# An integer cross attention regrouped by tile of queries inside a twelve-stage decoder kernel

## What is computed

```python
q = (x @ Wq + bq).reshape(1, B * N, H, hd)
kv = (cond @ Wkv + bkv).reshape(1, -1, 2, H, hd)
k, v = (kv[:, :, 0], kv[:, :, 1])
q = jnp.transpose(q * scale, (0, 2, 1, 3))        # k and v likewise
q = _fq_sym(q, axis=-1)                           # x / s rounded, clipped to +-127, times s
k = _fq_sym(k, axis=-1)                           # s = max|x| / 127 over the 16 columns
v = _fq_sym(v, axis=2)                            # over all tokens, per column
attn = softmax(einsum('bhqd,bhkd->bhqk', q, k))
attn = _fq_unsigned(attn, axis=-1)                # in steps of 1/255 of the row's maximum
out = einsum('bhqk,bhkd->bhqd', attn, v)
return out @ Wp + bp
```

## Time and profile before

| | us |
|---|---|
| median of 3 runs | 2005.1 (2003.45 to 2008.04) |
| profiled execution | 2004.22 |
| its span | 2002.9 |
| mean granted TensorE clock | 0.823 of full |
| stage `l1_cross`, from the start of its norm to the start of the next stage's | 642.3 to 953.8 |

### The profile page before, as it was taken

The page is one execution under the profiler, slowest core; times in us unless marked ns, Lnnn a source line. Parts: engine busy times, 40 slices in busy tenths (PEclk is TensorE's granted clock), DMA queues, the critical chain, the costliest instruction groups (busy, mean ns, idle before and its releaser), DMA issues. The chain is left out here.

```text
span 2002.9 us, 26899 instructions
## 1 busy us (share of the span) xinstructions
PE 1505.2 (75%) x8561; PEld 1049.0 (52%) x8564; DVE 1264.7 (63%) x3283; ACT 813.5 (41%) x2155; POOL 707.0 (35%) x969
## 2 busy tenths in 40 slices
PE   4899954799997558886884793035678769948998
PEld 3566643688886312223553462012456559935665
DVE  3677775455555778985335426988688679962222
ACT  1244421243342268883225213311577558821111
POOL 1488830166553436663001002425455312200000
PEclk8899986899998755556886896558799979968999
DMA  5000002100000035662200002010000020000000
GB/s 195 22 7 7 1 12 89 41 7 6 1 1 1 0 64 106 106 107 42 90 1 0 0 1 87 0 37 23 31 1 1 17 111 2 2 1 1 1 0 21
DMA packets 98380, 62.20 MB, mean 31 GB/s; under 512 B 88896, under 2 KB 93376, under 8 KB 96448
## 3 DMA queue, kind: packets, MB, share of 16 engines
q1 hardware_dynamic: 98240, 60.48, 11.3%
HBM read 38.44 MB, written 1.05 MB: 20 GB/s over the span
## 5 line engine op out<-in xcount | busy, mean ns | idle before, releaser
L101 PE MATMUL banks<-arena_a,normed_t 128*128 128x512 f32 (+3 forms) x736 | 282.5, 534 | 11.7 <-PEq L2983 11.7
L421 POOL TENSOR_TENSOR lut_weights<-lut_weights,arena_b 128x536 f32<-128x536 f32 x128 | 179.1, 1399 | 193.0 <-DVE arena_b L411 183.1
L101 PEld LDWEIGHTS banks<-arena_a,normed_t 128*128 128x128 f32 x736 | 140.3, 211 | 123.8 <-issue 120.4
L580 POOL TENSOR_SCALAR work<-work,small 128x256 f32<-128x256 f32 (+1 forms) x384 | 178.8, 483 | 73.9 <-DVE small L572 73.9
L101 PE MATMUL banks<-arena_a 64*128 64x512 bf16 (+1 forms) x384 | 161.7, 540 | 17.6 <-ACT arena_a L1483 9.3
L1483 ACT ACTIVATE arena_a<-banks,work 128x1024 uint8<-128x1024 f32 x128 | 154.0, 1203 | 39.3 <-DVE work L1428 28.7
L1426 DVE TENSOR_REDUCE work<-banks 128x1 f32<-128x1024 f32 x128 | 155.5, 1215 | 19.9 <-PE banks L101 19.9
L1513 POOL TENSOR_SCALAR arena_a<-arena_a 128x1024 bf16<-128x1024 uint8 x128 | 133.0, 1045 | 84.8 <-DMA arena_a<-arena_a 83.3
L107 PE MATMUL banks<-identity,work 128*128 128x128 f32 x968 | 133.3, 279 | 16.8 <-DVE work L1086 11.2
L560 ACT ACTIVATE work<-banks,small 128x256 f32<-128x256 f32 (+1 forms) x258 | 115.2, 458 | 62.3 <-DVE small L547 58.2
L107 PEld LDWEIGHTS banks<-identity,work 128*128 128x128 f32 x968 | 112.9, 145 | 31.5 <-DVE work L1086 12.2
(11 more groups left out here) (398 smaller groups left out, 3414.0 us busy)
## 6 DMA issues: line engine op xcount, KB each, us to landing
arena_a<-in_L3f_wg SPq DMA_DIRECT2D x1, 4096.0 KB, 12.4
arena_b<-in_lut_idx SPq DMA_DIRECT2D x8, 268.0 KB, 2.8
arena_b<-in_L_wqn SPq DMA_DIRECT2D x1, 2048.0 KB, 12.4
arena_b<-in_L_wo SPq DMA_DIRECT2D x1, 2048.0 KB, 16.5
arena_a<-in_L_wq SPq DMA_DIRECT2D x1, 2048.0 KB, 7.6
arena_a<-in_L_wo SPq DMA_DIRECT2D x1, 2048.0 KB, 13.6
arena_a<-arena_a SPq DMA_TRANSPOSE x128, 2.5
arena_a<-in_L_wgu SPq DMA_DIRECT2D x1, 2048.0 KB, 8.9
```

The source lines that it names most:

```text
L101: ins = t.matmul(out, lhs_t, rhs, start=start and i == 0, stop=stop and i == n - 1)
L421: g.tensor_tensor(o, o, lut_t[j % 2], ALU.add).then_inc(*summed.up(c * LUT + j))
L580: ins = g.tensor_scalar(e[:, c], e[:, c], A.rl[n % 2][:, 2 * hh + i:2 * hh + i + 1], 0.0, ALU.mult, ALU.add)
```

## The change

Only the stage `l1_cross` changes.

- `at(n)` is now `n // H, n % H`: a unit is still one tile and one head, but all 16 heads of one tile come first, then the next tile. All eight pairs of keys (`kt`) stay in SBUF; the queries are turned by tile (`query_slots`, two buffers).
- The output of a tile is made inside the loop. Behind the tile's last unit e: DVE norms all 16 heads in one operation at its step e + 8, PE turns the tile at e + 10, ACT copies it at e + 10, PE projects it at e + 12, DVE adds it to the residual and takes its statistics at e + 13. `OutputOfAll` and two of the four barriers are removed. The value scales are put on the rows of the projection weight instead of on the output.
- Head: PE makes the keys first, then turns the normed residual (ACT alone copies it), then makes queries, then values; DVE, ACT and POOL take keys first too. POOL spreads the queries behind all of its key work. Quotients are written as int16 and so rounded by the conversion, in place of the two operations with the large number. POOL's spreading now also clips the queries.
- All eight transposes of keys and the first of queries are issued by SP in front of the barrier; inside the loop one transpose of queries is issued per tile.
- Biases of keys, queries and output are added by a product of one row of ones with the bias row, behind the products of the weights.

The core of the diff:

```diff
         def at(n):
-            return n // (2 * NT), n // 2 % NT, 2 * (n // (2 * NT)) + n % 2
+            return n // H, n % H
+        def ended_at(n):
+            return n // H if 0 <= n < N and n % H == H - 1 else None
+        def projected(bank, x_t, b, w_, bias):
+            for i in range(TB):
+                ins = products(t, bank[:, i * D:(i + 1) * D], [(lhs(x_t, b * TB + i, k), w_(k)) for k in range(KH)] + [(ones[0:1, :], bias[0:1, :])])
+            return ins
...
         def tensor():
+            for b in range(NB):
+                projected(banks[b].f, ctx_t, b, lambda k: W["wkv4"][:, k * 512:k * 512 + D], W["bk4"]).then_inc(*ts.up(s, "k", b))
+            for b in range(NB):
+                t.wait_ge(*(yield normed_v, s, b))
+                t.wait_ge(*(yield normed_a, s, b))
+                token_turns(banks[4 + b].f, nf[:, b * CB:(b + 1) * CB], id_f).then_inc(*turned.up(s, b))
+            for b in range(NB):
+                t.wait_ge(*(yield xt_a, s, b))
+                projected(banks[4 + b].f, xt, b, lambda k: W["wq4"][:, k * D:(k + 1) * D], W["bq4"]).then_inc(*ts.up(s, "q", b))
...
-            for n in range(N + 7):
+            for n in range(N + 14):
...
+                if (i := ended_at(n - 10)) is not None:
+                    t.wait_ge(*(yield normed_o, s, i))
+                    turns(t, id_f, [(out_bank(i)[:, D + j * P:D + (j + 1) * P], oc[i % 2][:, j * P:(j + 1) * P]) for j in range(KH)]).then_inc(*o_in_psum.up(s, i))
+                if (i := ended_at(n - 12)) is not None:
+                    t.wait_ge(*(yield o_t_a, s, i))
...
+                    products(t, out_bank(i)[:, 0:D], [(ot[i % 2][:, j * P:(j + 1) * P], wp[j]) for j in range(KH)] +
+                             [(ones[0:1, :], W["bp4"][0:1, :])]).then_inc(*out_made.up(s, i))
...
         def vector():
+                v.tensor_tensor(heads(ki[b % 2]), heads(banks[b].f), each(r1), ALU.mult).then_inc(*vs.up(s, "k", b))
+                if b >= 2:
+                    v.wait_ge(*(yield as_, s, "split", b - 2))
+                v.tensor_scalar(kv[b % 2], ki[b % 2], 127.0, -127.0, ALU.min, ALU.max).then_inc(*vs.up())
+                v.tensor_tensor(heads(kv[b % 2]), heads(kv[b % 2]), each(s1), ALU.mult).then_inc(*vs.up(s, "keys", b))
...
+                if (i := ended_at(n - 8)) is not None:
+                    v.wait_ge(*(yield exped, s, n - 8))
+                    v.reciprocal(rl[i % 2], ls[:, i * H:(i + 1) * H]).then_inc(*vs.up())
+                    v.wait_ge(*(yield mixed, s, n - 8))
+                    v.tensor_tensor(heads(oc[i % 2]), heads(out_bank(i)[:, 0:D]), each(rl[i % 2]), ALU.mult).then_inc(*normed_o.up(s, i))
+                if (i := ended_at(n - 13)) is not None:
+                    v.wait_ge(*(yield out_made, s, i))
+                    x_i = x[:, i * D:(i + 1) * D]
+                    v.tensor_tensor(x_i, out_bank(i)[:, 0:D], x_i, ALU.add).then_inc(*added.up(s, i))
+                    v.bn_stats(stat[:, 6 * i:6 * i + 6], x_i).then_inc(*vs.up())
+                    v.bn_aggr(mv[:, 2 * i:2 * i + 2], stat[:, 6 * i:6 * i + 6]).then_inc(*vs.up())
...
         def scalar():
+            for b in range(NB):
+                a.wait_ge(*(yield turned, s, b))
+                a.copy(*copied_t(b, banks[4 + b].f)).then_inc(*xt_a.up(s, b))
+            for b in range(NB + 1):
+                if b < NB:
+                    for n in range(3):
...
+                    as_.all(s, "split", b)
+                if b:
+                    z = b - 1
+                    a.wait_ge(*(yield ts, s, "v", z))
+                    a.activation(vtf[:, z * 512:(z + 1) * 512], banks[z].f, ACT.Identity, bias=W["bv4"][:, z // 2:z // 2 + 1]).then_inc(*as_.up(s, "v", z))
+            for k in range(KH):
+                a.activation(v16[k], vtf[:, k * 1024:(k + 1) * 1024], ACT.Identity, scale=rv[:, k:k + 1]).then_inc(*as_.up(s, "rounded", k))
...
+                if (i := ended_at(n - 10)) is not None:
+                    a.wait_ge(*(yield o_in_psum, s, i))
+                    a.copy(ot[i % 2], out_bank(i)[:, D:2 * D]).then_inc(*o_t_a.up(s, i))
...
         def sync():
-            yield MEET
-            turn_pair(0)
+            sp.wait_ge(*(yield as_, s, "split", NB - 1))
+            turn_keys(0)
+            sp.wait_ge(*(yield gs, s, "spread", 0))
+            turn_queries(0)
+            for pr in range(1, H // 2):
+                turn_keys(pr)
+            yield MEET
             for n in range(N):
-                if n % (2 * NT) == 4 and pr + 1 < H // 2:
...
-                    turn_pair(pr + 1)
+                if h == 4 and i + 1 < NT:
+                    if i:
+                        sp.wait_ge(*(yield scored, s, i * H - 1))
+                    turn_queries(i + 1)
```

More of the change, by code:

```diff
@@ L1369, in vector @@
[L1369 removed]
+            yield from norm_vector(s, nf)
             for b in range(NB):
[L1371 to L1399 removed]
@@ L1408, in vector @@
[L1408 to L1419 removed]
+                s1, r1 = sc[b][:, 0:32], sc[b][:, 32:64]
@@ new lines, in vector @@
+                v.wait_ge(*(yield ts, s, "k", b))
+                v.tensor_reduce(s1, heads(banks[b].f), AX.X, ALU.max, apply_absolute_value=True).then_inc(*vs.up())
+                v.wait_ge(*vs.now())
+                v.tensor_scalar(s1, s1, 1.0 / 127.0, 1e-8, ALU.mult, ALU.max).then_inc(*vs.up())
+                v.wait_ge(*vs.now())
+                v.reciprocal(r1, s1).then_inc(*vs.up())
+                v.wait_ge(*vs.now())
+                v.tensor_tensor(heads(ki[b % 2]), heads(banks[b].f), each(r1), ALU.mult).then_inc(*vs.up(s, "k", b))
@@ L1458, in scalar @@
-            for b in range(NB):
-                for n in range(3):
-                    if n == 0:
-                        a.wait_ge(*(yield vs, s, "keys", b))
-                    else:
-                        a.wait_ge(*(yield gs, s, "rest", b, n - 1))
-                    for i in range(TB):
-                        a.copy(slots4(kx, b * TB + i)[:, :, :, n, :], pairs(kt_[b % 2] if n else kv[b % 2], i)).then_inc(*as_.up())
-                    as_.all(s, "part", b, n)
-                as_.all(s, "split", b)
@@ new lines, in scalar @@
+            a.wait_ge(*(yield loaded[4], "all"))
+            for b in range(NB + 1):
+                if b < NB:
+                    for n in range(3):
+                        if n == 0:
+                            a.wait_ge(*(yield vs, s, "keys", b))
+                        else:
+                            a.wait_ge(*(yield gs, s, "rest", b, n - 1))
+                        for i in range(TB):
+                            a.copy(key_slots(b * TB + i)[:, :, :, n, :], pairs(kr[b % 2] if n else kv[b % 2], i)).then_inc(*as_.up())
+                        as_.all(s, "part", b, n)
+                    as_.all(s, "split", b)
[3 more added lines that the diff above has]
+                    a.activation(vtf[:, z * 512:(z + 1) * 512], banks[z].f, ACT.Identity, bias=W["bv4"][:, z // 2:z // 2 + 1]).then_inc(*as_.up(s, "v", z))
```

323 lines of the change are left out of this document (108 added, 215 removed).

## The result

The changed kernel takes **1985.8 us** (1985.2 to 1986.5, 4 runs) against 2004.4 beside it (2003.5 to 2008.0): ratio 0.9904, 95% interval 0.9887 to 0.9921. It is faster by 18.5 us where 57.5 were forecast, and the time lies outside the range of 1938 to 1958. The profiled execution has a span of 1985.0 us at a mean clock of 0.820.

A forecast was written before the change was run, and what follows sets the result against it. The prediction took SP's queue to bound the old loop, with head and end chains of waits. Gains of 31.6 (head), 0.4 (loop) and 25.5 (end) sum to 57.5 us, from 2004.2 to 1947; range 1938 to 1958.

The forecast's parts named there:

- What bounds the old kernel: Old loop: SP's queue of transposes is the bound, 25.1 us per 16 units; DVE is next at 23.0.
- The products of the loop: Loop: three fp32 products per tile take PE 1.28 us, making DVE wait 1.3; the loop gains only 0.4 us.
- The bounds named: Loop: 186.4 us if the products were wholly covered; some 10 more if SP's lag broke through.
- rival B: Loop: products hidden or cheap, 7 x 1.3 = 9 us less, total 1938; 12%.
- The end: After the last reduction R: last norm at R + 7.4, end at R + 11.4, against 36.9 before; gain 25.5 us.
- The key phase of the head: Head: 24 fp32 key products on PE, 4.5 us at half clock, then full, done at 649.8.
- Rival D: Head longer: clock stays at half (+4) and port contention on the split chain (4 x 1), total 1955; 9%.
- The split chain: Head: ACT and POOL split four key batches, 5.17 us each, plus two value copies, from 652.6 to 674.5.
- The stretching of DVE beside POOL: Head: two operations of each late query batch stretched by 0.64; DVE chain ends near 689 instead of 687.
- Rivals C: Loop longer: SP's lag and PE's new waits add up, 1.5 us a tile, 10 us, total 1957; 20%.
- E: Loop: PE's waits empty the pipeline at every tile, seven times 10 us, slower than before at 2017; 3%.
- F: Head: new order brings nothing because the chain of splits is as slow as the old one, total 1978; 1%.

The follow-up runs named there:

- a4: Kernel before, but keys turned only for the first two pairs (later pairs use stale keys): 1996.6 us, ratio 0.9955.
- c2: Changed kernel, output bias added by POOL in the head, loop projection in bf16: 1964.7 us. Its law: the step is the insertion plus 1.43.
- a3: Changed kernel without the biases of keys and queries, their 16 one-row products left out: 1964.2 us, ratio 0.9797.
- a1: Changed kernel with each bias added by a full-height product (128 rows of 1/128, bias in every partition) instead of one row: 1965.8 us, ratio 0.9795.
- d2: Changed kernel with the head's bias products of keys and queries over 64 rows instead of one: 1983.8 us, ratio 0.9892.
- e1: Changed kernel with the loop's score products over all 128 rows instead of 64 (not the reference's function): 1983.3 us, ratio 0.9900.
- b1: Changed kernel, output bias added by POOL in the head, each tile's projection cut into four pieces of 64 columns in four units: 1989.0 us, ratio 0.9918.

## Why the prediction was wrong

**What bounds the old kernel: right** (a4).

**The products of the loop: the term that was mis-sized.** The step "three fp32 products of 256 columns, 3 x 0.427" (1.28) took the records of the earlier trace rows for products (eight in 3.38, which are four products). They are passes, two for each fp32 product; with six passes and the height change it is 3.15. Put into the law of c2, 1.28 gives 2.71, the forecast's step of 2.7; 3.15 gives the 4.57 that came. Seven times 1.87 are 13.1 of the loop's 13.4. All else of this step came as told: the steps of 1.38, the norm's 2.00 (1.95), the add's 2.40, SP off the limit. The bounds named ("if the products were wholly covered") and rival B lay on the wrong side: nothing of the insertion is covered, and the forecast's own wait of 1.3 was its 1.28 uncovered too.

**The end.** To the last norm it took 7.29 us (R + 7.4 forecast). Turn, copy, products and add to 932.97 took 4.9 where 3.0 was forecast; the products (929.30 to 932.55) had 3.25 in place of 1.5. That is the whole 1.8.

**The key phase of the head, two mistakes.** Forecast 7.4 us (to 649.8), measured 25.2. The first is the same count: a3 and a1 put the right one at 9.3 + 3.4 = 12.7. The second is the assumption that the clock rises as it did in the old head: it didn't. It was 0.50 from 639.5, where PE stood idle, to 670.2, and the height changes are the cause (12.5 us, a1 and d2). Of these, 8 x 0.29 = 2.3 are the changes by themselves (3.15 a tile against 2.86 of full height at half clock, 732.39 to 735.25 in a1), the rest the clock. Rival D had the clock at half, but for +4 us, because it priced it on half of the passes, and it had no mechanism.

**Behind the keys.** The split chain began 18.4 late (671.0 for 652.6) and took 25.6 in place of 21.9, 4.5 of it ACT's wait for the value product (685.73), which stood behind the queries' bias products on PE. SP's nine transposes took 13.3 (13.4 forecast) and stood last, as told. From there to the first reduction it was 1.9, not 1.4. The clip of int16 took 0.41 and 0.43 for 1024 columns, inside its bounds. The stretching of DVE beside POOL, for which the prediction drew on the Trainium skill's page "SBUF — State Buffer", section "Who interferes with whom", is in the trace: L1403 takes 0.18 alone and 0.61 beside POOL's spreading. It cost nothing, as DVE's and ACT's chain ended at 709.4 and SP at 710.0.

**Rivals C, E and F** didn't come. What did come was none of them: a count of passes, shared by all the cases, and a clock that stayed low, which the range couldn't take in.

**What stays open:** why height changes keep a low clock low but left a full one full, and what the loop's clock waits for beyond them (0.59 in e1, though all heights but one were equal, and 0.53 in a1, though they weren't). That DVE's wait behind the projection could be hidden by scores stored further ahead wasn't tried.

## What to carry to other kernels

Before pricing a product from a record, divide the records of one line by the products its code issues: here an fp32 product was two records, a transpose one. Operations put into PE's in-order queue, ahead of scores that DVE waits for, cost this loop their whole length at each insertion, even with PE's slack of e1. So shorten them (bf16: 3.42 to 1.96 a step; here with less precision) rather than cut them into pieces. A bias as a one-row product isn't cheap: a full-height one with the bias in every partition saved 20 us in all.

## What the runs showed of the hardware

- At half clock, six fp32 passes of 256 columns took 3.15 us where the last two had 1 or 64 rows, 2.86 where they had 128. In the head, products of one height let the clock rise to 2.4 GHz in the second tile of keys (a1, at 646.8); alternating heights kept it at 1.2 GHz through all eight tiles, 25 us, with 64 rows as with one. Once it was full, the same alternation left it full for the 13.5 us of the queries.
- At half clock a single fp32 weight load lasts 0.32 us (mean of 112 in b1; 0.19 at full clock in a1), one of bf16 0.11 (c2). Loads overlap one another: four of fp32 fill 0.93, two of bf16 0.13. The Trainium skill, page "TensorE: Matmul & The Clock Gate", section "Weight-path perf modes — Fast Weight Load (FWL) and DoubleRow", has a fast load for 128 weights of any type but FP32; the traces agree that bf16 loads are the shorter. At half clock an fp32 pass of 64 columns took 0.26 us (b1), most of it filled by loads; one of 256 columns 0.42 (eight in 3.38), and 0.50 where a change of height follows four of them.
- Even score products of 64 rows between mixes of 128 cost PE 0.2 us a unit over the same work at one height (1.28 against 1.08).
